# Where ScalarE copies the attention sums out of their bank, and how the maxima are spread over the gated stage

## The reference

```python
xn = _layernorm(x, axis=-1)
scores = jnp.einsum('bqhd,bkhd->bhqk', q, k) * scale        # 32 heads of 16
scores = scores + alibi[None, :, None, :]
scores = jnp.where(causal[None, None, :, :], scores, jnp.float32(-1000000000.0))
attn = jax.nn.softmax(scores, axis=-1)
s = jnp.einsum('bhqk,bkhd->bqhd', attn, v).reshape(B, S, D)  # then w_out, b_out
h = jax.nn.silu(gate) * up                                   # ternary octonion weights
g = _silu(oct_ternary_linear(h, w_down))
x = x + s * g
```

## Time and profile before

| | |
|---|---|
| median of three runs | 889.02 us (886.86 to 889.53) |
| the profiled execution | 884.88 us, span from first to last instruction 883.0 us |
| mean granted PE clock | 0.986 of 2.4 GHz |
| PE busy | 92% of the span |
| DVE busy | 72% |
| ACT busy | 53% |
| POOL busy | 14% |

### The profile page before, as it was taken

The page is one execution under the profiler, slowest core; times in us unless marked ns, Lnnn a source line. Parts: engine busy times, 40 slices in busy tenths (PEclk is TensorE's granted clock), DMA queues, the critical chain, the costliest instruction groups (busy, mean ns, idle before and its releaser), DMA issues.

```text
span 883.0 us, 16119 instructions
## 1 busy us (share of the span) xinstructions
PE 815.3 (92%) x5938; PEld 354.8 (40%) x5938; DVE 639.5 (72%) x1818; ACT 471.4 (53%) x615; POOL 120.5 (14%) x136
## 2 busy tenths in 40 slices
PE   5799989999999999999899999999999899998997
PEld 4345434444444434334333333333333333333333
DVE  5375786743433555664799999999999999996556
ACT  4443265333132222222378887877788788778540
POOL 3123131323032122122000000000000005500000
PEclk9999998999999999999799999999999999999999
DMA  7735321248401100100111222221215223543645
GB/s 219 215 108 173 126 84 72 96 116 254 165 1 71 72 1 25 71 1 25 72 44 56 65 75 76 64 75 52 65 55 168 82 74 114 183 128 122 187 150 204
DMA packets 72591, 88.40 MB, mean 100 GB/s; under 512 B 26926, under 2 KB 39214, under 8 KB 72000
## 3 DMA queue, kind: packets, MB, share of 16 engines
q1 hardware_dynamic: 72384, 87.10, 31.1%
q0 software_dynamic: 128, 0.27, 0.2%
HBM read 51.15 MB, written 35.93 MB: 99 GB/s over the span
## 4 chain that ended last, share of the span: by engine, by line
PE 68%; DVE 17%; issue 7%; DMA 5%; ACT 2%; SPq 0%; POOL 0%; ACTq 0%; DVEq 0%
PE psum L1463 13%; PE psum L1423 9%; PE psum L1486 9%; PE psum L1487 9%; DVE mshown L1137 5%; PE psum L1497 4%; DVE mx L1141 4%; PE psum L1498 4%; PE psum L1439 4%; PE psum L1323 2%; PE psum L1325 2%; PE psum L1324 2%; PE psum L1337 2%; PE psum L1335 2%; PE psum L1336 2%
## 5 line engine op out<-in xcount | busy, mean ns | idle before, releaser
L869 ACT ACTIVATE probs<-psum,exp_scale 128x1024 f32<-128x1024 f32 (+1 forms) x320 | 312.7, 1027 | 93.6 <-PE psum L1448 56.5
L1137 DVE CUSTOM_DVE_ANT_0 mshown<-psum,ahead 128x384 bf16<-128x384 f32 (+3 forms) x512 | 221.9, 487 | 14.9 <-PE psum L1423 13.7
L1423 PE MATMUL psum<-QKs 51*128 51x512 f16 (+3 forms) x768 | 195.0, 333 | 18.4 <-DVE mx L1137 7.3
L1463 PE MATMUL psum<-probs,Vs 128*32 128x512 f32 (+3 forms) x1536 | 162.1, 510 | 16.4 <-ACT osum L875 16.2
L1141 DVE TENSOR_REDUCE mx<-psum 128x1 f32<-128x512 f32 x256 | 158.4, 682 | 2.7 <-PE psum L1423 1.7
L1439 PE MATMUL psum<-QKs 53*128 53x512 f16 (+3 forms) x768 | 139.9, 331 | 2.2 <-DMA QKs<-mrows 1.6
L1486 PE MATMUL psum<-X,room 128*128 128x512 f16 (+1 forms) x352 | 133.9, 380 | 0.0
L1487 PE MATMUL psum<-X,room 128*128 128x512 f16 (+1 forms) x352 | 133.4, 379 | 0.0
L1423 PEld LDWEIGHTS psum<-QKs 51*128 51x128 f16 x768 | 53.2, 94 | 169.0 <-DVE mx L1137 88.9
L894 ACT ACTIVATE room<-psum,gate_half 128x512 f32<-128x512 f32 (+1 forms) x44 | 30.2, 687 | 109.9 <-PE psum L1487 109.9
L1171 DVE SCALAR_TENSOR_TENSOR room<-room,psum 128x512 f32<-128x512 f32 (+1 forms) x44 | 30.2, 687 | 67.6 <-ACT room L894 67.6
(11 more groups left out here) (158 smaller groups left out, 911.6 us busy)
## 6 DMA issues: line engine op xcount, KB each, us to landing
o_scr<-osum SPq DMA_DIRECT2D x32, 256.0 KB, 2.4
QKs<-q_scr SPq DMA_DIRECT2D x96, 64.0 KB
QKs<-k_scr SPq DMA_DIRECT2D x96, 64.0 KB
q_scr<-qk_stage SPq DMA_DIRECT2D x16, 256.0 KB, 2.2
k_scr<-qk_stage SPq DMA_DIRECT2D x16, 256.0 KB, 2.2
v_scr<-v_stage SPq DMA_DIRECT2D x16, 256.0 KB, 2.0
Vs<-v_scr SPq DMA_DIRECT2D x16, 256.0 KB
probs<-in_L_attn_x SPq DMA_DIRECT2D x4, 1024.0 KB, 11.4
```

The source lines that it names most:

```text
L869: nc.scalar.activation(probs[n % PSLOTS][:, 2 * pair:2 * pair + 2, 0:COLS[n]], s_bank[pair][:, :, 0:COLS[n]], ACT.Exp, scale=exp_scale[:, ...
L1137: last = nc.vector.tensor_tensor_reduce(out=mshown[at % 2][:, cols], in0=m_bank[bank][:, cols], in1=ahead[:, CH - keys:], scale=1.0, scala ...
L1423: last = nc.tensor.matmul(tile[:, hh, :], Qs[s][rows, pair + hh, qb * P:(qb + 1) * P], Ks[s][rows, pair + hh, k0:k0 + keys], start=(hh == ...
L1463: last = nc.tensor.matmul(pv_bank[32 * h:32 * h + 32, CH - cols:CH], Vs[s][:, kb, h::QH], probs[n % PSLOTS][:, h, at:at + cols], start=(kb ...
```

## The change

Two edits. ACT's copies get their place in the common list from the products: `copy_out` stands where `("products", t, 2)` and `("products", t, 9)` stand, instead of behind the exponentials named above. And the early maxima of the gated stage are given out only when three are due (or at the last tile), so that they stand in runs of three behind every third tile. The list of the attention stage is the same as before for PE, DVE and SP.

```diff
@@ work_order
         due = max(n + 1 - F_FIRST, 0) * len(early) // (len(tiles) - F_FIRST)
-        order += [("maximum", *x) for x in early[given:due]]
-        given = max(given, due)
+        if due - given >= MRING or n + 1 == len(tiles):
+            order += [("maximum", *x) for x in early[given:due]]
+            given = due
@@ scalar
                     t, n, pair = w[1:]
                     exponential(t, n, pair)
-                    if pair == 1 and n == LAG - 2 and t > 0:
-                        copy_out(t - 1, 1, ENDS[1])
-                    if pair == 1 and n == ENDS[0] + LAG - 1:
-                        copy_out(t, 0, ENDS[0])
+                if w[0] == "products" and w[2] in ENDS:
+                    copy_out(w[1], ENDS.index(w[2]), w[2])
@@
-            copy_out(QUADS - 1, 1, ENDS[1])
```

## The result

| | before | after |
|---|---|---|
| median | 888.87 us (886.86 to 889.53, 4 runs) | 863.22 us (862.08 to 863.99, 4 runs) |
| the profiled execution | 884.88, span 883.0 | 863.99, span 862.1 |
| after / before | | 0.9728, interval 0.9701 to 0.9755 |

The forecast was 865 in a range of 859 to 875, and the measured gain is 24.2 us by the ratio (21.8 to 26.6). Measured again beside two experiments the changed kernel gave 0.9698 (0.9669 to 0.9727).

A forecast was written before the change was run, and what follows sets the result against it. PE bounds the gated stage; in attention PE and DVE take turns waiting. 884.88 - 13.7 (copy) - 9.9 (runs) = 861.3 us for an execution like the profiled one; 865 as median, timed runs lying higher; range 859 to 875.

The forecast's parts named there:

- what the copy gives: Attention: chunk 0's copy one exponential earlier removes DVE's idling for fills in 15 groups, 13.7 us in all.
- The margin of DVE over the fill: Attention, fill behind step 3's products: DVE could read it at 574.1 but is ready at 574.32, so DVE binds by 0.2 us.
- The bound above: Attention: the earlier copy of chunk 0 can give at most PE's whole wait for osum, 16.2 us.
- rival (b): Attention: the stall moves, PE at the fill or the late exponentials bind, half the gain is kept, 872 us; chance 0.09.
- (c): The gated stage's edit gives nothing or is given back, 875 us; or attention's edit gives nothing, 879 us; chance 0.06.
- The copy of the last sum: Attention: moved ahead of step 1's exponentials, it makes them 0.18 us late but covered; costed at nothing, 2.7 us without cover.
- The runs: Gated stage's second half: three maxima together cost 0.62 us against 1.24 singly; 17 runs save 9.9 us after scaling.
- serial rival (a): Gated stage: the maxima of a run don't overlap, saving 6.8 us instead of 9.9, 868 us in all; chance 0.08.
- the drain's price: Gated stage: each change between 128 and 51 rows costs PE about 0.10 us, taken as draining the array.
- The end of chunk 2: Gated stage, first down tile: slack before PE needs POOL's part falls from 1.96 to about 0.8 us; cost nothing.
- PE's wait behind the last four maxima: End of the gated stage: PE's 3.17 us idle time stays the same, and the clock drop behind it is expected to stay.
- signs of being wrong: Changed profile: DVE waits for PE elsewhere, ACT waits before a copy, PE idles at chunk 2's first down tile, more clock drops.

The follow-up runs named there:

- two experiments: The changed kernel with LEAD = 14 and with LEAD = 17 in place of 11, more early maxima of group 1 in the gated stage: 1.0112 and 1.0153 of before.
- the sorted kernel: Changed kernel with 18 maxima of 512 columns sorted so that a run's three fills use the same half of the rows; one run, 862.43 us.

## Why the prediction was right

**Where attention waited, and what the copy gives.** Right at every step: the copy starts when the products end, PE starts the next products without waiting, DVE binds, and the group behind is today's, moved. PE's waits for `osum` are gone and DVE's too. The margin of DVE over the fill, 0.2 us by the prediction, is 562.87 - (562.34 + 0.37) = 0.16. The term was sized slightly low: 0.91 us a group (13.7 in all) where the spans show 1.02 (15.3). Most of what is missing is in the rows: DVE's idle time counts from the end of the short instruction behind a read, but a read that does not have to wait starts together with it, 0.08 us before that end. A stall costs its idle time and that lost overlap, 13.7 + 15 x 0.08 = 14.9 us; the other 0.4 are open. The bound above, PE's 16.2, holds. The rival (b), half of the gain, is out by the groups' 24.25 us, and (c) by the two kernels with one edit each.

**The copy of the last sum.** Costed at nothing, and shown to be nothing by the kernel in which it alone is moved. The exponentials start at 553.05, one slot of 0.47 us behind the copy, as worked out.

**The runs.** 9.9 us forecast, 9.7 by the stretch's length, 9.5 by the kernel with the runs alone. The four-fill row of before priced the run exactly: 0.62 us. That two fills overlap, and that it takes different halves, is shown by the sorted kernel. The serial rival (a) is thereby out. The changes between 128 and 51 rows cost 0.10 us each: a single maximum of 128 columns costs 0.25 us and one of 512 costs 0.41, which is 384 columns' time apart, and a pair costs as much as a single. What these 0.10 us are made of is not separated. The prediction calls them the drain's price, but the weight loads of the kernel before, around the maximum of the earlier trace rows, allow another reading:

```profile
332.05 0.10 PEld L1487 LDWEIGHTS psum<-X,room 128*128 128x128 f16 x1
332.57 0.09 PEld L1423 LDWEIGHTS psum<-QKs 51*128 51x128 f16 x1 [0.42 <-DVE mx L1141]
332.89 0.10 PEld L1486 LDWEIGHTS psum<-X,room 128*128 128x128 f16 x1 [0.23 <-issue]
```

Between tiles a load starts one matmul ahead of its own: the first of these is for the matmul at 332.26. Across a change it starts only with its own matmul, at 332.57 and at 332.89, and it takes 0.09 to 0.10 us, as much as the change costs. The semaphore on such a load is not the reason: where two tiles of the changed kernel meet without a maximum, the load has one too and starts ahead, at 339.86 for the matmul at 340.08. In a run of fills on one half (the sorted kernel) the loads are ahead again. Whether the change costs a drain or an uncovered load, no run here tells. The prediction's estimate of 0.05 us for a change is half of the measured price; it turns the 128 cycles of the Trainium skill's "TensorE: Matmul & The Clock Gate", Single matmul latency, into time at the upper clock, while the section splits up the latency at the lower one.

**The end of chunk 2.** Worked out at 0.8 us of remaining slack. The changed kernel's POOL ends the last part at 342.43 + 1.15 = 343.58, and PE needs it at 344.39, 0.81 us later:

```profile
342.43 1.15 POOL L745 TENSOR_TENSOR room<-room 80x512 f16<-80x512 f32 x1 [2.10 <-ACT room L900]
```
```profile
344.39 0.38 PE L1495 MATMUL psum<-room 80*128 80x512 f16 x1
```

**The rest.** PE's wait behind the last four maxima stayed at 3.2 us, and the clock fell behind it as before. The tail got no faster; instead the rows of group 15's maxima landed 1.4 us later in the profiled execution. This wait was 2.1, 1.2 and 1.7 us in the kernels with the copies alone, the first copy alone and the changed one again, and 3.9 with the runs alone, whose groups are those of before: it varies with neither edit. What it varies with I have not followed, and I had not priced it.

Two of the prediction's signs of being wrong did appear, both outside what its sum prices. The clock is down in one stretch more, in the first stage, as told above. And ACT waits in front of a copy, 3.2 us in 3 pieces in all:

```profile
798.36 0.60 ACT L876 ACTIVATE osum<-psum 128x512 f32<-128x512 f32 x1 [0.62 <-PE psum L1461]
813.22 0.60 ACT L876 ACTIVATE osum<-psum 128x512 f32<-128x512 f32 x1 [1.34 <-PE psum L1461]
```

The third, of 1.22 us before the last copy, was there before. All three lie in group 15 or behind it, none in the 15 groups that the sum goes by.

**The sum.** 861.3 was worked out for an execution like the profiled one, 865 for the median; 863.2 was measured. The difference between the two, 4.1 us, was taken from before's own runs, and it did not repeat: the changed kernel's profiled execution, 863.99, is the slowest of its four, while before's was faster than all four of its timed runs. That the median came so close is luck in part. From 861.3 to that execution's 863.99 there are 3.2 us more in the first stage, 0.9 more behind group 15's rows and 0.2 more in the gated stretch, less the 1.6 that attention gave above the 13.7.

## What to carry to other kernels

A copy that frees a bank belongs in its engine's list where its input is done. Too late and too early both can cost: chunk 0's copy one exponential late was 1.02 us a group, the last sum's copy one exponential early 0.76. What counts of a wait is who stands next: PE's 16.2 us were worth 15.3 because DVE, near full, waited behind it. The last sum's copy stood two exponentials late, nobody waited for it, and moving it was worth nothing.

Small matmuls with few rows that are strewn between full ones are cheaper in neighbours on different halves of the rows, up to the number of banks in their ring: two for the price of one, a fourth for a wait. A row of such a run anywhere in the old trace prices it before anything is changed.

A shift of a hand-made order by a few items is not neutral because the counts agree: with three items moved, a group went from 24.25 to 26.21 us.

## What the runs showed of the hardware beyond that

- Two matmuls of 512 columns on partitions 0 to 50 and 64 to 114 of the array's rows take 0.39 us together, as one does, and two on the same half 0.22 more. The banks are not what differs: the three fills of a run go to three banks in both kernels.
- Where PE's matmuls change between 128 and 51 rows, the next weight load does not start ahead of its matmul, and each change costs 0.10 us.
- DVE's reads in a row overlap by 0.08 us each, and idle time in a profile leaves that out.
- The lower level of PE's clock comes at other places of the first stage from execution to execution: between 45 and 50 us the granted clock was 1.00 in the kernel before and 0.66 in the changed one. The gated stretch starts between 294.2 and 297.8 us in seven profiles, counted back from the stretch's last matmul, and that is about as much as the runs of one kernel differ; the clock is part of it.
